# Layer 1 of a two-layer attention kernel: output product from rounded parts, and the values' bias moved to the output's

## What is computed

```
xn = layernorm(x)
qkv = xn @ W_in.T + b_in                      # 16 heads of 64
attn = softmax(q/8 . k + q/8 . k_dist)
out = attn @ v + attn . v_dist                # per head, 1024 channels in all
s = out @ W_out.T + b_out                     # the output product
g = silu(sqrt((x' cos)^2 + (x' sin)^2))       # x' = xn, 256 x 256 tables
x = x + s * g
```

## Time and profile before

| | us |
|---|---|
| runs, median (lowest to highest) | 1291.83 (1291.41 to 1296.13) |
| profiled execution, its own time | 1301.92 |
| its span | 1300.0 |
| TensorE busy | 1204.6 |
| VectorE busy | 866.6 |
| ScalarE busy | 672.8 |
| GpSimd busy | 592.9 |

### The profile page before, as it was taken

How to read it: one execution, slowest core, us unless ns; L and a number is a source line. 1 busy time by engine, 2 the same in 40 slices (tenths; PEclk the granted TensorE clock), 3 DMA queues, 4 the chain that set the end, 5 groups by cost and what they waited for, 6 DMA issues and landing times. The chain is left out here.

```text
span 1300.0 us, 33870 instructions
## 1 busy us (share of the span) xinstructions
PE 1204.6 (93%) x13840; PEld 751.4 (58%) x13840; DVE 866.6 (67%) x1896; ACT 672.8 (52%) x1297; POOL 592.9 (46%) x611
## 2 busy tenths in 40 slices
PE   5888999999999999999975999999999999999997
PEld 4423444343433434434334878787878788787876
DVE  5766676777776777666644666668575766667665
ACT  2455667565565665656662444444444453444453
POOL 2065577675676676667743322313131423323131
PEclk9588999999999999999996999999999999999999
DMA  7634445344354434345222001010100101010100
GB/s 194 134 79 99 102 82 129 88 111 111 78 119 98 110 87 102 90 92 114 112 63 87 3 3 50 4 50 4 50 4 10 43 3 50 4 50 4 33 4 18
DMA packets 57994, 86.74 MB, mean 67 GB/s; under 512 B 8304, under 2 KB 38256, under 8 KB 57840
## 3 DMA queue, kind: packets, MB, share of 16 engines
q1 hardware_dynamic: 57840, 84.58, 26.9%
HBM read 50.40 MB, written 33.55 MB: 65 GB/s over the span
## 5 line engine op out<-in xcount | busy, mean ns | idle before, releaser
L1140 POOL TENSOR_TENSOR room<-room 128x512 f32<-128x512 f32 x248 | 309.0, 1278 | 172.4 <-ACT room L817 172.4
L976 DVE TENSOR_REDUCE negmax<-s_bank 128x1 f32<-128x512 f32 x512 | 330.3, 679 | 66.5 <-PE s_bank L670 66.5
L817 ACT ACTIVATE room<-t_bank 128x512 f32<-128x512 f32 x512 | 282.4, 593 | 111.3 <-PE t_bank L680 107.6
L680 PE MATMUL t_bank<-qst,kst 50*128 50x512 f32 x512 | 210.3, 474 | 25.3 <-ACT room L817 22.9
L670 PE MATMUL s_bank<-kst,qst 48*128 48x512 f32 x512 | 216.6, 490 | 6.1 <-DVE negmax L976 3.7
L680 PEld LDWEIGHTS t_bank<-qst,kst 50*128 50x128 f32 x512 | 84.0, 189 | 148.7 <-ACT room L817 93.1
L1853 POOL TENSOR_TENSOR win<-rt,apart 128x512 f32<-128x512 f32 x32 | 41.9, 1331 | 232.0 <-DVE rt L1683 232.0
L693 PE MATMUL a_bank<-room,v 128*32 128x512 f32 x1024 | 142.0, 628 | 0.7
L1840 POOL TENSOR_TENSOR ex<-ex,rc 128x256 f32<-128x256 f32 x64 | 41.8, 654 | 142.7 <-DVE rc L1711 142.7
L1429 PE MATMUL pr<-xt_h,win_h 128*128 128x512 f32 x256 | 106.2, 415 | 0.8 <-issue 0.8
L1429 PE MATMUL pr<-xt_h,win_l 128*128 128x512 f32 x256 | 100.9, 394 | 0.0
(11 more groups left out here) (247 smaller groups left out, 2296.8 us busy)
## 6 DMA issues: line engine op xcount, KB each, us to landing
park<-qk_h SPq DMA_DIRECT2D x128, 128.0 KB, 2.4
qst<-park SPq DMA_DIRECT2D x64, 192.0 KB, 3.8
kst<-park SPq DMA_DIRECT2D x64, 192.0 KB, 4.4
park<-qk_l SPq DMA_DIRECT2D x64, 128.0 KB, 2.4
room<-in_x SPq DMA_DIRECT2D x8, 512.0 KB, 3.8
xr<-in_x SPq DMA_DIRECT2D x8, 512.0 KB, 4.7
room<-x SPq DMA_DIRECT2D x8, 512.0 KB, 3.9
out<-so SPq DMA_DIRECT2D x32, 128.0 KB, 1.7
```

The lines of the kernel that those rows point to most:

```text
L680: pe.matmul(t_bank[w % 2][:, :], kst[slot][rows, j, c * P:(c + 1) * P], qst[slot][rows, j, :], start=True, stop=True).then_inc(m.t_done, 1)
L817: act.activation(probs[:, c, j, :], t_bank[w % 2][:, :], ACT.Exp, scale=SCALE0).then_inc(m.exp_done, 1)
L976: dve.tensor_reduce(negmax[:, i_par, 2 * odd + j, c:c + 1], s_bank[S_BANK[w]][:, :], X, ALU.max, negate=True).then_inc(m.max_done, 1)
L1140: add = pool.tensor_tensor(sums[:, pair, h, :], probs[:, 2 * pair, h, :], probs[:, 2 * pair + 1, h, :], ALU.add)
```

## The change

- The output weights `wout` are split once into `wout_h` (ScalarE, rounded copy of 128 x 2048) and `wout_l` (VectorE, the rest), at the start of layer 1.
- ScalarE copies each AV rounded into `ot_h`, without the bias. VectorE gets `low_outputs(i, k)`: `ot_l` = AV in PSUM less `ot_h`, 128 x 512, in step k + 2, for pair 6 behind `transposed_blocks(7)` and for pair 7 three sums by distance later. AV(k) waits for `low_outputs(k-1)` where it used to wait for ScalarE's copy.
- Each output product of a tile and head pair becomes three: `ot_h` x `wout_h`, `ot_h` x `wout_l`, `ot_l` x `wout_h`.
- TensorE's order at the tail is new: pairs 0 to 6 of tiles 1 and 2, pair 7 of tile 1, first transposes, pair 7 of tile 2, tile 0, second transposes, pairs 0 to 6 of tile 3, transposes of `pd`, pair 7 of tile 3, closing products. VectorE does both `low_parts` of the next block behind `distances`.
- The values' bias: as the weights of a row sum to one, it goes through the output weights once (eight fp32 products in block 0, into the other half of `fin`) and is added to `bout`.
- Places in the shared room move (`wout` to the lower part; `ot` becomes `ot_h`, `ot_l` and `ot_l1_late`).

```diff
--- before.py
+++ after.py
@@ TensorE, block 0, ahead of Q0
                         for hp in range(HP):
-                            mm = pe.matmul(fin[:, 0:E], vdx[:, hp, :], wout[:, hp, :], start=(hp == 0), stop=(hp == HP - 1))
+                            pe.matmul(fin[:, 0:E], vdx[:, hp, :], wout[:, hp, :], start=(hp == 0), stop=(hp == HP - 1))
+                        for hp in range(HP):
+                            mm = pe.matmul(fin[:, E:2 * E], bqkv[:, 2 * HP + hp:2 * HP + hp + 1].to_broadcast([P, P]),
+                                           wout[:, hp, :], start=(hp == 0), stop=(hp == HP - 1))
                         mm.then_inc(m.g_psum, 1)
@@ TensorE, AV
-                        wait(pe, m.ot_ok, HP * i + k)
+                        wait(pe, m.ot_low, HP * i + k)
@@ TensorE, the output product
-                for n, t in enumerate(W_ORDER):
...
+                def outputs(t, pairs):
+                    for hp in pairs:
+                        tokens = slice(t * P, (t + 1) * P)
+                        for n, (x, w) in enumerate(((ot_h[:, hp, tokens], wout_h), (ot_h[:, hp, tokens], wout_l),
+                                                    (ot_l(hp)[:, tokens], wout_h))):
+                            pe.matmul(w_bank(t)[:, 0:E], x, w[:, hp, :], start=(hp == 0 and n == 0), stop=False)
+
+                first_pairs, last_pair = range(HP - 1), (HP - 1,)
+                pe.wait_ge(m.wout_low, 1)
+                pe.wait_ge(m.ot_low, HP * i + HP - 1)
+                for t in (1, 2):
+                    free_pr(i, "W", t)
+                    outputs(t, first_pairs)
+                pe.wait_ge(m.ot_low, HP * (i + 1))
+                outputs(1, last_pair)
+                if not last:
+                    transposes(i + 1, 0)
+                outputs(2, last_pair)
+                if first:
+                    pe.wait_ge(m.bout_ok, 1)
+                wait(pe, m.so_ok, TT * i)
+                outputs(0, range(HP))
+                if not last:
+                    transposes(i + 1, 1)
+                outputs(3, first_pairs)
+                pe.wait_ge(m.pd_ok, 2 * (i + 1))
+                misc_free()
+                for u in range(TT):
+                    mm = pe.transpose(misc[:, u * P:(u + 1) * P], pd[:, u, :, :].rearrange("p h r -> p (h r)"), ident[:, :])
+                mm.then_inc(m.pd_psum, 1)
+                prev_misc[0] = ("PD", i, 0)
+                outputs(3, last_pair)
                 pe.wait_ge(m.pdt_ok, i + 1)
@@ ScalarE, ahead of the blocks
+            act.wait_ge(m.u_load, 16 * shared.U_LOADS)
+            act.activation(wout_h[:, :, :], wout[:, :, :], ACT.Copy).then_inc(m.wout_high, 1)
@@ ScalarE, AV
-                        act.activation(ot[:, k, :].rearrange("p (t q n) -> p t q n", t=TT, q=BLOCKS),
-                                       o_ps[:, :, 0:TT * BLK].rearrange("p q (t n) -> p t q n", t=TT), ACT.Identity,
-                                       bias=bqkv[:, 2 * HP + k:2 * HP + k + 1]).then_inc(m.ot_ok, 1)
+                        act.activation(ot_h[:, k, :].rearrange("p (t q n) -> p t q n", t=TT, q=BLOCKS),
+                                       o_ps[:, :, 0:TT * BLK].rearrange("p q (t n) -> p t q n", t=TT),
+                                       ACT.Copy).then_inc(m.ot_ok, 1)
@@ VectorE
+            def low_outputs(i, k):
+
+                dve.wait_ge(m.ot_ok, HP * i + k + 1)
+                if i == 0 and k == 0:
+                    dve.wait_ge(m.wout_low, 1)
+                dve.tensor_tensor(ot_l(k).rearrange("p (t q n) -> p t q n", t=TT, q=BLOCKS),
+                                  o_ps[:, :, 0:TT * BLK].rearrange("p q (t n) -> p t q n", t=TT),
+                                  ot_h[:, k, :].bitcast(F32).rearrange("p (t q n) -> p t q n", t=TT, q=BLOCKS),
+                                  ALU.subtract).then_inc(m.ot_low, 1)
+
+            def value_bias():
+
+                dve.wait_ge(m.g_ok, 3)
+                dve.tensor_tensor(bout[:, :], bout[:, :], fin[:, E:2 * E], ALU.add).then_inc(m.bout_ok, 1)
...
+            dve.wait_ge(m.wout_high, 1)
+            dve.tensor_tensor(wout_l[:, :, :], wout[:, :, :], wout_h[:, :, :].bitcast(F32), ALU.subtract).then_inc(m.wout_low, 1)
...
+                if i == 0:
+                    value_bias()
...
                     if k >= 1:
                         transposed_blocks(i, k - 1)
+                    if k >= 2:
+                        low_outputs(i, k - 2)
...
                 key_sums(i, HP - 1)
                 transposed_blocks(i, HP - 1)
+                low_outputs(i, HP - 2)
+                by_distance(i, 1, range(3))
+                low_outputs(i, HP - 1)
+                by_distance(i, 1, range(3, NREL))
+                distances(i)
                 if not last:
                     low_parts(i + 1, 0)
-                by_distance(i, 1, range(NREL))
-                distances(i)
-                if not last:
                     low_parts(i + 1, 1)
```

More of the change, by code:

```diff
@@ L55 @@
 HP = H1 // 2
+OT_EARLY = 5
 NREL = 8
@@ L176, in __init__ @@
             (4, HG, S), (2, HG, S), (HALF, S), (QT, E), (QT, E))
-        low, self.ot, self.q2, self.th, self.wout, self.sq, self.kt = rooms(
-            (KC * 3 * H1 * D1,), (HP, TOK), (TT, E), (TT, E), (HP, E), (2, 2 * E), (2, TOK))
+        low, late, self.q2, self.th, _, self.sq, self.kt = rooms(
+            (KC * 3 * H1 * D1,), (HP * TOK,), (TT, E), (TT, E), (HP * E,), (2, 2 * E), (2, TOK))
         self.pt = [low[:, i * TOK // 2:(i + 1) * TOK // 2].rearrange("p (h t k) -> p h t k", h=2, t=TT) for i in range(2)]
-        self.xn1, self.xr1, self.xt1 = [low[:, i * KC * 2 * E:(i + 1) * KC * 2 * E] for i in range(2, 5)]
-        self.vdx = self.ot[:, 4:6, :].rearrange("p a b -> p (a b)").rearrange("p (h c) -> p h c", h=HP)
+        self.xn1, self.xr1, self.xt1 = [low[:, TOK + i * TT * E:TOK + (i + 1) * TT * E] for i in range(3)]
+        early = TOK + 3 * TT * E
+        self.wout = low[:, early:early + HP * E].rearrange("p (h c) -> p h c", h=HP)
+        self.vdx = late[:, 4 * TOK:4 * TOK + HP * P].rearrange("p (h c) -> p h c", h=HP)
+        part = 4 * KC * H1 * D1
+        self.ot_h = at("ot_h1", [P, HP, TOK], F32R, room_at + part * 3)
+        self.ot_l = at("ot_l1", [P, OT_EARLY, TOK], F32R, room_at + 4 * early)
+        self.wout_h = at("wout_h1", [P, HP, E], F32R, room_at + 4 * (KC * 3 * H1 * D1 + HP * TOK + 2 * TT * E))
+        self.wout_l = at("wout_l1", [P, HP, E], F32R, stacks_at + part * 3)
         self.ones = sb("ones", [P, P])
@@ L1274, in layer1 @@
         cs_h, cs_l = shared.cs_h, shared.cs_l
-        wout = shared.wout
+        wout, wout_h, wout_l = shared.wout, shared.wout_h, shared.wout_l
         gk = shared.gk
@@ L1296, in layer1, with ot_l @@
         pt = shared.pt
-        ot = shared.ot
+        ot_h, ot_l_late = shared.ot_h, sb("ot_l1_late", [P, HP - OT_EARLY, TOK], F32R)
+        def ot_l(k):
+            return shared.ot_l[:, k, :] if k < OT_EARLY else ot_l_late[:, k - OT_EARLY, :]
         r15, rt = sb("r15", [P, H1, TT, 2 * NREL - 1]), sb("rt", [P, H1, TT, NREL])
@@ L1347, in layer1 @@
         m.ot_ok = sem("ot_ok1")
+        m.ot_low = sem("ot_low1")
+        m.wout_high = sem("wout_high1")
+        m.wout_low = sem("wout_low1")
+        m.bout_ok = sem("bout_ok1")
         m.f_psum = sem("f_psum1")
```

## The result

| | before | after |
|---|---|---|
| runs, median us (lowest to highest, runs) | 1292.69 (1291.41 to 1296.13, 4) | 1319.14 (1317.59 to 1324.20, 4) |
| profiled execution, its own time | 1301.92 | 1320.22 |
| its span | 1300.0 | 1318.0 |

The ratio is 1.0207, with a 95% interval of 1.0172 to 1.0242: the changed kernel is 26.5 us slower. The forecast was 1317 us, 25 us slower. Its steps do not all stand, though: one term was far too large and one cost was left out of it, and the two nearly cancel.

The account below looks back on a forecast made before the run. TensorE's own back-to-back work was taken to bound layer 1. Seven blocks at 1.9 + 2.1 - 1.0 = 3.0 (21.0), 0.7 in the last and 3.3 once gave 25 us: 1291.83 becomes 1317 us, range 1302 to 1333.

Parts of the forecast that it names:

- The pace: Output products on TensorE: each rounded 256-column product takes 0.125 us, 96 take 12.0 us a block instead of 13.8.
- Part 1: Block tail on TensorE: second transposes come 10.3 us behind AV7 instead of 8.24, 2.1 us more.
- Part 2: Second transposes to closing products: ScalarE's unchanged list takes 7.05 us, TensorE idles about 3; stretch shrinks from 8.04, gaining 1.0.
- Part 3: Low parts of the outputs on VectorE: AV7 waits for AV6's low part and starts 1.9 us later a block.
- VectorE's lag: Steps after step 2: each falls behind by 0.29 us, 1.4 us by the last key sums.
- The upper end given there, 2.3: AV7's start: 2.3 us later if no idle time on VectorE takes anything in.
- Part 4: Once, at layer 1's start: eight fp32 bias products add 3.3 us; weight split and bias addition add nothing.
- The clock: TensorE's granted clock: expected at 1.00 throughout layer 1, so no cost in the sum.
- rival (a): Clock falls behind the changed block's idles, costing 12 to 24 us in seven blocks, 1329 to 1341 us; chance 0.2.
- The argument against it: Against a falling clock: the changed block's idle of 3 us is shorter than the 3.44 us seen in layer 0.
- The last block: AV7 to closing products, without token transposes: 13.9 us instead of 15.14, 1.2 less; with AV7's 1.9, 0.7 in all.

Follow-up runs that it names:

- the two reorderings: Two separate edits of the changed kernel: ScalarE's square root and tanh before the copies of transposed tokens, 1288.88 us; TensorE's first and second transposes earlier, 1289.37 us.
- both orders changed: Changed kernel with TensorE's transposes earlier and ScalarE's copy of AV6 before the third square, together: 1280.99 us, ratio 0.9891 to the kernel before.

## Why the prediction was right, and where it was not

**The pace** stands: 0.120 us from product to product, taken as 0.125, a term 5 ns too large for each of 72 or 96. The Trainium skill (TensorE: Matmul & The Clock Gate, Back-to-back issue gap) gives an estimate of 0.109; the trace does not agree with it.

**Part 1** stands: the second transposes are 1.7 us later behind AV7, forecast 2.1; the difference is the pace (72 x 0.005 = 0.36).

**Part 2** stands: 7.00 us behind the second transposes, forecast 7.05; idle 3.1, forecast about 3; released by the copy of pdt, and shown to be ScalarE's chain by the two reorderings.

**Part 3** had the right mechanism and the wrong size. AV7 waits 1.0 us a block, and comes 0.8 later, not 1.9: from the closing products to AV7 block 4 takes 59.64 us with 3.0 of clock in it (1008.49 to 1068.13) and block 5 takes 58.39 with 1.7, against 55.89 before (1000.61 to 1056.50). The failed term is the 1.4 us of VectorE's lag, which is 0.1 in the trace. It was summed as if every other instruction kept its duration, but the sums by distance and the normalisation moved out from beside GpSimd and gave 1.0 back; with the low part behind them the lag is 1.1. A lag of 0.1 in the prediction's own chain, 1056.27 + 0.1 + 0.76 against 1056.50, gives 0.6. The upper end given there, 2.3, is too low by the prediction's own figures: without any idle time each of five steps would lose 0.61 - 0.08 = 0.53, 2.65 in all, and AV7 would come 3.2 later. Nothing in the sum goes by it.

**Part 4** stands. The bias products of the changed kernel, behind those with the value distances:

```profile
714.09 3.62 PE L1499 MATMUL o_ps<-room 128*128 128x256 f32 x16
717.55 3.62 PE L1501 MATMUL o_ps<-room,bqkv 128*128 128x256 f32 x16
720.82 0.58 PE L1445 MATMUL pr<-xt_h,win_h 128*128 128x512 f32 x1
```

717.55 to 720.82 is 3.27 us, forecast 3.3. The split of the weights and the addition to `bout` were hidden.

**The clock** is what the sum left out. It was held at 1.00 throughout layer 1 and given a chance of 0.2 as rival (a), priced at 12 to 24 us. It came, at 13.2 by the windows and 10.8 by the experiment that fills the idle, the low end of its price. The argument against it, that 3.1 us is shorter than the 3.44 us of the earlier trace rows, carried nothing: the prediction had no row with an idle near 3 us ahead of a stretch at full clock. The Trainium skill (TensorE: Matmul & The Clock Gate, Why this matters for your kernels) says that idle gaps between bursts bring the slower clock; behind the 3.1 us the trace agrees.

**The last block** took 13.46 us from AV7 to the closing products, 1.7 less than before; forecast 1.2.

The sum with the measured terms: AV7 8 x 0.8 = 6.4, the second transposes 7 x 1.7 = 11.9, the stretch behind them 7 x -1.04 = -7.3, the last block -1.7, once 3.3, the clock 13.2, in all 25.8 against 26.5 by the runs and 24.8 by the two traces. Without the clock it is 12.6: the forecast's 25 came true because 8.8 too much for AV7 (8 x 1.9 against 6.4), 2.8 for the second transposes and 0.8 for the two stretches behind, 12.4 in all, stand against the missing 13.2 of clock. That they cancel is luck. The time was right; two of its terms were not.

Open: what decides whether the clock falls behind an idle, as 3.1 us did not always bring it and 1.2 us sometimes did; and why a fall costs 3.0 us in some blocks and 1.7 in most. In the changed kernel's block with 3.0, and in one block with the copy of AV6 moved and two with the low part moved that lost as much, the clock had fallen before the closing products started.

## What to carry to other kernels

When TensorE's work between two points shrinks, look for the in-order list of another engine that the work used to cover, and move what starts that list (here two transposes) earlier by as much as is saved. An idle of some 3 us on TensorE mostly costs more than its length, because the clock behind it falls: count it, or fill or cut it. If an instruction is put into a full list, look at which neighbours of other engines everything behind it now meets; durations are not constants.

## What was not expected of the hardware

- Idles of TensorE before the closing products, seven in each kernel: 3.1 us, the granted clock fell behind 7 of 7; 2.4 us, 3 of 7; 1.7 us, 0 of 7. With ScalarE's copy of AV6 moved, and with the low part moved, idles of 3.1 us had it in 5 of 7 each. Idles of 1.2 to 1.4 us in the middle of a block had it once in each of three kernels (square root and tanh first, 24 added products, both orders changed), and one of 1.22 in the kernel before had not. A fall cost 1.7 us, in some blocks 3.0. Extra products that nobody reads made a kernel 10.8 us faster.
- A 128x256 sum on VectorE with two SBUF inputs takes 0.47 us alone and 0.70 beside a GpSimd instruction of the same size; a 128x512 subtraction that reads PSUM keeps 0.65 to 0.69.
- A product of 128 x 128 with 128 x 256 takes 0.120 us with rounded inputs and 0.433 in fp32, so three rounded ones cost 0.36, less than one in fp32.
